# A two-layer graph block on one core: score cross terms without matmuls of their own, and another order of each round

## The reference

```
for k in (0, 1):                       # h starts as x
    a     = softmax(h @ h.T / sqrt(384), axis=-1)
    delta = a * adj
    attn  = delta / (delta.sum(-1, keepdims=True) + 1e-10)
    hl, hs, hr = h @ Wl.T + bl, h @ Ws.T + bs, h @ Wr.T + br
    ctx   = (attn * upper) @ hl + diag(attn)[:, None] * hs + (attn * lower) @ hr
    h     = relu(layernorm(ctx, 1e-12) * gain + shift)
out = layernorm(x + h, 1e-5)
```

## Time and profile before

| | |
|---|---|
| time, median of 3 runs | 1630.99 us (1630.69 to 1631.91) |
| the profiled execution | 1631.82 us, of which 1630.1 from its first to its last instruction (the span) |
| granted clock of TensorE | 0.997 of full speed |
| busy share of the span | PE 98%, PEld 98%, DVE 86%, ACT 66%, POOL 74% |
| DMA | 179 MB in 463,943 packets |

### The profile page before, as it was taken

How to read it: one execution, slowest core, us unless ns; L and a number is a source line. 1 busy time by engine, 2 the same in 40 slices (tenths; PEclk the granted TensorE clock), 3 DMA queues, 4 the chain that set the end, 5 groups by cost and what they waited for, 6 DMA issues and landing times.

```text
span 1630.1 us, 35740 instructions
## 1 busy us (share of the span) xinstructions
PE 1605.1 (98%) x9509; PEld 1597.9 (98%) x9509; DVE 1398.9 (86%) x4368; ACT 1078.0 (66%) x2835; POOL 1212.5 (74%) x1542
## 2 busy tenths in 40 slices
PE   8999999999999999999999999999999999999996
PEld 7899999999999999999999999999999999999995
DVE  7788888888888888888888888888888888888886
ACT  6566666666666666666666666666666666666654
POOL 5677777777777777777777777777777777777764
PEclk9999999999999999999999999999999999999998
DMA  5444444444444444444444444444444444444431
GB/s 175 102 110 107 114 114 107 111 107 116 107 114 111 110 107 113 114 107 112 107 115 106 114 112 110 109 110 115 107 114 109 112 106 114 114 108 111 108 93 45
DMA packets 463943, 179.17 MB, mean 110 GB/s; under 512 B 348592, under 2 KB 462896, under 8 KB 463920
## 3 DMA queue, kind: packets, MB, share of 16 engines
q1 hardware_dynamic: 463920, 178.91, 43.3%
HBM read 112.92 MB, written 65.86 MB: 110 GB/s over the span
## 4 chain that ended last, share of the span: by engine, by line
PE 92%; DMA 1%; DVE 1%; SPq 1%; POOL 1%; ACT 1%; issue 1%; DVEq 0%; POOLq 0%; ACTq 0%
PE p_proj L430 70%; PE p_gather L517 16%; PE p_score L424 5%; PE p_score L446 1%; DMA rows_mem<-rows_blocks 1%; SPq L366 1%; DMA attnT_whole<-attn_mem 1%; SPq L351 0%; POOL rstd L1173 0%; POOL attnT L1163 0%; DVE stats L623 0%; POOL attnT_split L1169 0%; DVE p_gather L646 0%; DVE p_gather L619 0%; DVE rows_blocks L725 0%
## 5 line engine op out<-in xcount | busy, mean ns | idle before, releaser
L430 PE MATMUL p_proj<-w,hT_layer 128*128 128x384 f32 x6912 | 1368.6, 339 | 0.9 <-DVE w L744 0.5
L430 PEld LDWEIGHTS p_proj<-w,hT_layer 128*128 128x128 f32 x6912 | 1162.5, 188 | 2.0 <-POOL w L1220 1.0
L281 POOL TENSOR_TENSOR proj_split<-proj,proj_split 128x768 fp32r<-128x768 f32 x253 | 467.6, 1848 | 182.3 <-ACT proj_split L943 181.9
L517 PE MATMUL p_gather<-proj_split,attnT_split 128*128 128x384 f32 x1536 | 309.3, 335 | 2.3 <-POOL attnT_split L1169 1.6
L1173 POOL TENSOR_TENSOR rstd<-veps,neg_half 128x1 f32<-128x1 f32 x384 | 206.8, 549 | 91.9 <-DVE veps L632 82.6
L517 PEld LDWEIGHTS p_gather<-proj_split,attnT_split 128*128 128x128 f32 x1536 | 269.9, 188 | 4.7 <-POOL attnT_split L1169 2.7
L943 ACT ACTIVATE proj_split<-proj 128x768 fp32r<-128x768 f32 x256 | 214.9, 839 | 84.7 <-DVE proj L688 83.7
L688 DVE TENSOR_TENSOR proj<-p_proj,bias_all 128x768 f32<-128x768 f32 x256 | 244.9, 957 | 12.9 <-PE p_proj L430 5.1
L1169 POOL TENSOR_TENSOR attnT_split<-attnT,attnT_split 128x256 fp32r<-128x256 f32 x256 | 190.3, 743 | 71.0 <-ACT attnT_split L934 70.9
L947 ACT ACTIVATE o<-y,nbias,rstd 128x384 f32<-128x384 f32 x128 | 90.7, 709 | 227.0 <-POOL nbias L1177 227.0
L424 PE MATMUL p_score<-hT_layer 128*128 128x256 f32 x768 | 216.6, 283 | 1.8 <-DVE rows L720 0.8
(11 more groups left out here) (59 smaller groups left out, 1598.3 us busy)
## 6 DMA issues: line engine op xcount, KB each, us to landing
xt_raw<-xT SPq DMA_DIRECT2D x128, 192.0 KB, 2.6
xn<-x SPq DMA_DIRECT2D x128, 192.0 KB, 2.4
out<-o SPq DMA_DIRECT2D x128, 192.0 KB, 2.0
rows_mem<-rows_blocks SPq DMA_DIRECT2D x124, 192.0 KB, 1.9
rowsT<-rows_mem SPq DMA_DIRECT2D x496, 48.0 KB, 2.4
adj_layer<-adj SPq DMA_DIRECT2D x256, 64.0 KB, 1.9
attn_mem<-attn_blocks SPq DMA_DIRECT2D x124, 128.0 KB, 1.7
attnT_whole<-attn_mem SPq DMA_DIRECT2D x496, 32.0 KB, 2.2
```

Source lines behind the costliest of these rows:

```text
L281: op.tensor_tensor(proj_split[u][:, LO], proj[u][:, UP:LOW + 1, :], proj_split[u][:, HI].bitcast(F32), ALU.subtract).then_inc(s_proj_lo[k], 1)
L430: return nc.tensor.matmul(p_proj[:, which, 0:D], hT_of(k, b)[:, slot, st, c, :], w[:, k, which, mv, c, :], start=(n == 0), stop=(n == 8))
L517: last = nc.tensor.matmul(home(k, b)[:, 0:D], AT_split[u][:, st, side, :], proj_split[u][:, mv, side, :], start=(side == UP and n == 0), s ...
```

## The change

TensorE no longer transposes the high-by-low part of the scores. The scores of layer 1 (now of graph i + 2) and of layer 2 (graph i - 2) stand together in its list, one behind each projection step of layer 1's self part (pair_slice), and share one PSUM bank. ScalarE copies both LO parts in one instruction (copy_cross) and both HI parts to free columns of other banks (keep_high). VectorE block-transposes the LO parts of both layers (turn_cross), and they go through DRAM beside the attention of both: the store and the four loads carry four blocks for each row (store_swap, load_swap) instead of two. In the next round GpSimd adds the part and its transpose (add_cross), and then VectorE scales the scores of both layers, one behind the other. The first graphs and the last three of layer 2 keep the cross matmul (11 of 256).

The order of the rounds is another one as well. VectorE adds layer 1's bias ahead of the scaling and layer 2's ahead of the output rows. Layer 2's gather stands nine projection steps later. GpSimd's layer-1 root stands ahead of the cuts. ScalarE has both exponentials behind normalise_rows and ahead of high_sides of layer 2. SP takes xn first and the adjacency tiles last. The input's high and low parts have four slots instead of two, the output's sums, means and roots two instead of one. The core of the diff:

```diff
-        E = [p_score[0][:, 2, :], p_score[1][:, 2, :]]
+        parts = [p_score[0][:, 0:2, :], p_score[0][:, 2:4, :]]
+        cross_parts = p_score[0].rearrange("p (k t) n -> p k t n", t=2)[:, :, LO, :]
+        E = [p_score[1][:, 0, :], p_score[1][:, 1, :]]
         p_rows = bank("p_rows", [P, 4, N])
-        ident_p = [p_score[0][:, 3, :], p_score[1][:, 3, :]]
-        attn_mem = [nc.dram_tensor(f"attn_mem_{slot}", (P, 2, N), F32, kind="Internal").ap() for slot in range(2)]
+        ident_p = p_score[1][:, 2, :]
+        kept = [p_rows[:, 3, :], p_gather[0][:, D:D + N]]
...
+                if b0 is not None and 2 <= n < 2 + C:
+                    step = score_step(0, b0, slot0, n - 2)
+                    if n == 1 + C:
+                        step.then_inc(s_parts[0], 1)
+                if n == 2 + C:
+                    done(pe, s_lo[1], b1)
+                if 2 + C <= n < 2 + 2 * C:
+                    step = score_step(1, b1, slot1, n - 2 - C)
+                    if n == 1 + 2 * C:
+                        step.then_inc(s_parts[1], 1)
...
-                    score0 = (0, i + 1, q) if live(i, i + 1) else None
-                    project_sides(0, i, p, 1, i - 4, range(18), score0)
-                    project_self(0, i, p, 1, i - 4)
+                    b0 = i + 2 if live(i, i + 2) else None
+                    project_sides(0, i, r, 1, i - 4, range(18))
+                    project_self(0, i, r, 1, i - 4, pair=(b0, (r + 2) % 4, i - 2, p))
+                    project_sides(1, i - 3, q, 0, i, range(9))
                     gather(1, i - 4)
-                    project_sides(1, i - 3, q, 0, i, range(18), (1, i - 2, p))
+                    project_sides(1, i - 3, q, 0, i, range(9, 18))
                     project_self(1, i - 3, q, 0, i)
-                    gather(0, i)
+                    gather(0, i, True)
...
+                if live(i, i + 2):
+                    nc.vector.transpose(blocks[:, slot, 2:4].rearrange("p k n -> p (k n)"),
+                                        crossed[:].rearrange("p k n -> p (k n)")).then_inc(s_cross_blocks, 1)
+                else:
+                    nc.vector.transpose(blocks[:, slot, 3], crossed[:, 1]).then_inc(s_cross_blocks, 1)
...
                 low_rows(i - 2, p)
+                add_bias(0, i, True)
+                if not isinstance(i, int) or i > 4:
+                    done(dve, s_cross_sum, i - 5)
+                    done(dve, s_kept, i - 5)
+                    output_mean(i - 5, q)
+                    if live(i, i + 1):
+                        scaled_scores(0, i + 1, q, kept[0], cross_sum[:, 0])
+                    scaled_scores(1, i - 3, q, kept[1], cross_sum[:, 1])
+                if not direct_rows(i, i - 1):
+                    block_rows(i - 1)
+                if live(i, i + 1):
+                    mask(i, 0, i + 1, q)
                 mask(i, 1, i - 3, q)
-                if live(i, i + 1):
-                    done(dve, s_score[0], i + 1)
                 diagonal(1, i - 3, q)
                 if live(i, i + 1):
-                    scaled_scores(0, i + 1, q)
-                add_bias(0, i, True)
-                block_rows(i - 1)
-                if live(i, i + 1):
-                    mask(i, 0, i + 1, q)
                     diagonal(0, i + 1, q)
+                turn_cross(i, p)
                 add_bias(0, i, False)
                 row_moments(1, i - 4, p)
                 row_variance(1, i - 4, p).then_inc(s_veps[1], 1)
                 centre_layer2(i, i - 4)
+                add_bias(1, i - 3, True)
                 output_rows(i - 4, p)
-                done(dve, s_score[1], i - 2)
-                add_bias(1, i - 3, True)
-                scaled_scores(1, i - 2, p)
-                output_mean(i - 4)
                 add_bias(1, i - 3, False)
...
+            def copy_cross(i):
+                if live(i, i + 2):
+                    done(act, s_parts[0], i + 2)
+                    done(act, s_parts[1], i - 2)
+                    nc.scalar.activation(crossed[:], cross_parts, ACT.Copy).then_inc(s_crossed, 1)
+                else:
+                    done(act, s_parts[1], i - 2)
+                    nc.scalar.activation(crossed[:, 1], cross_parts[:, 1], ACT.Copy).then_inc(s_crossed, 1)
+            def keep_high(i):
+                if live(i, i + 2):
+                    nc.scalar.activation(kept[0], parts[0][:, HI, :], ACT.Copy)
+                nc.scalar.activation(kept[1], parts[1][:, HI, :], ACT.Copy).then_inc(s_kept, 1)
...
                 relu_rows(i, i - 2, p)
-                if live(i, i + 1):
-                    cross_scores(0, i + 1)
                 high_rows(i - 2, p)
-                high_sides(1, i - 4)
                 normalise_rows(i, i - 1)
+                exponentials(1, i - 3, q)
                 if live(i, i + 1):
                     exponentials(0, i + 1, q)
+                high_sides(1, i - 4)
+                copy_cross(i)
+                high_projections(0, i)
                 high_sides(0, i)
-                high_projections(0, i)
-                if live(i, i + 2):
-                    high_input(i + 2, p)
+                keep_high(i)
+                if live(i, i + 3):
+                    high_input(i + 3, (r + 3) % 4)
                 if live(i, i + 1):
                     squared_denominators(0, i + 1, q)
                 squared_denominators(1, i - 3, q)
                 if live(i, i - 5):
                     output_squares(i - 5, q)
-                cross_scores(1, i - 2)
-                if live(i, i - 5):
                     finish(i, q)
                 high_projections(1, i - 3)
-                exponentials(1, i - 2, p)
...
+            def add_cross(first, last):
+                nc.gpsimd.tensor_tensor(cross_sum[:, first:last], crossed[:, first:last],
+                                        whole[:, 2 + first:2 + last], ALU.add).then_inc(s_cross_sum, 1)
...
                 low_projections(nc.gpsimd, pool, 1, i - 4)
                 attn_arrived(i - 1, q)
+                if not isinstance(i, int) or i > 4:
+                    add_cross(0, 2)
+                deviation_layer1(i - 1)
                 cut_sides(1, i - 4)
-                deviation_layer1(i - 1)
                 low_sides(1, i - 4)
                 cut_sides(0, i)
                 low_sides(0, i)
                 low_projections(nc.gpsimd, pool, 0, i)
                 deviation_layer2(i - 4)
                 if live(i, i - 5):
-                    deviation_output(i - 5)
-                if live(i, i + 2):
-                    low_input(i + 2, p)
+                    deviation_output(i - 5, q)
+                if live(i, i + 3):
+                    low_input(i + 3, (r + 3) % 4)
...
-                store_attn(i, p)
-                if live(i, i - 3):
-                    done(sp, s_y, i - 5)
-                    sp.dma_start(xn[:, q], x[i - 3]).then_inc(s_xn[q], 16)
+                if not isinstance(i, int) or 3 <= i < G:
+                    store_swap(i, p)
                 if live(i, i - 1) and not direct_rows(i, i - 1):
                     load_rows(i, i - 1, q)
                 if closing(i) and live(i, i - 4):
                     done(sp, s_side[1], i - 4)
-                load_attn(i, p)
+                if not isinstance(i, int) or 3 <= i < G:
+                    load_swap(i, p)
```

More of the change, by code:

```diff
@@ L99, in graph_block @@
         AT_split = [sb(f"attnT_split{k}", [P, 2, 2, N], F32R) for k in (1, 2)]
-        A_blocks = sb("attn_blocks", [P, 2, 2, N])
-        AT_whole = sb("attnT_whole", [P, 2, N])
+        crossed = sb("crossed", [P, 2, N])
+        cross_sum = sb("cross_sum", [P, 2, N])
+        blocks = sb("blocks", [P, 2, 4, N])
+        whole = sb("whole", [P, 4, N])
         rows_blocks = sb("rows_blocks", [P, D])
@@ new lines, in load_swap @@
+            def load_swap(i, slot):
+                first, last = swapped(i)
+                sp.wait_ge(s_swap_out[slot], swap_moves(i, slot))
+                pieces = swap_mem[slot].rearrange("(r a) k (s b) -> s a k r b", a=B, b=B)
+                for s in range(4):
+                    rows_s = slice(s * B, (s + 1) * B)
+                    if last - first == 1:
+                        sp.dma_start(whole[rows_s, first, :].rearrange("a (r b) -> a r b", b=B),
+                                     pieces[s][:, first]).then_inc(s_swap_in[slot], 16)
+                    else:
+                        sp.dma_start(whole[rows_s, first:last, :].rearrange("a k (r b) -> a k r b", b=B),
+                                     pieces[s][:, first:last]).then_inc(s_swap_in[slot], 16)
@@ L464, in project_sides, with project_self @@
                     last.then_inc(s_proj[k], 1)
-            def project_self(k, b, slot, before, b_last, scored=None, first=0, last_part=8):
+            def project_self(k, b, slot, before, b_last, scored=None, first=0, last_part=8, pair=None):
                 done(pe, s_self_biased[before], b_last)
@@ L471, in project_self @@
```

(4 more changed lines are left out.)

334 lines of the change are left out of this document (188 added, 146 removed).

## The result

The changed kernel takes **1697.61 us** (median of 4 runs, 1693.9 to 1699.05), the kernel before 1631.45 beside it (4 runs, 1630.69 to 1633.79): a ratio of 1.040, interval 1.038 to 1.042. It is slower. The profiled execution took 1693.9 us, 62 more than that of before; it is the quickest of the four, so the profile explains these 62 us and not the 66 between the medians.

The account below looks back on a forecast made before the run. TensorE bounds the kernel at 12.44 us a round; relieved to 12.2, it yields to GpSimd's own ring (12.7) and memory's (12.6). Taken as 12.72, +0.28 x 123 = +34.4 on 1631.0 gives 1665 us, range 1612 to 1712.

Parts of the forecast that it names:

- two rings of hand-overs: Waiting chains from one add_cross to the next: GpSimd's own, forecast 12.7 us a round, and one through memory, about 12.6.
- seven of nine: Steps of the ring through memory, from add_cross to the next, forecast to come to about 12.6 us together.
- the ring through memory: add_cross, exponentials, masks, turn_cross, store, loads, landing, next add_cross: forecast 12.3 to 12.7 us, about 12.6, not deciding.
- GpSimd's own: Ring of GpSimd's steps and its waits for ScalarE, add_cross to add_cross: forecast 12.7 us a round, deciding.
- the rival, the alternation of scores and single projections: On TensorE: forecast 0 to 0.2 us a round, taken as 0; as rival in spread_scores 0.1, no chance given.

Follow-up runs that it names:

- finish_only: Changed kernel with only high_projections of layer 2 moved ahead of the output row on ScalarE; 1684.91 us, 1.033 against the kernel before.
- two_row_loads: Changed kernel with two of the four loads of layer 1's rows left out, nothing else; 1649.93 us, 1.011 against the kernel before.
- swap_turn_finish: Changed kernel with layer 1's exponential first (its tile in SBUF), turn_cross ahead of both diagonals, high_projections of layer 2 ahead of the output row; 1610.14 us, 0.988.
- before_no_cross: Kernel before the change with its cross matmuls left out and nothing moved; 1605.16 us, 0.984.
- spread_scores: swap_turn_finish with scores spaced out, layer 1's behind projections 5, 7, 9 of its sides, layer 2's behind 2, 4, 6 of its self part; 1624.74 us, 0.996.

## What to carry to other kernels

When two rings of hand-overs come out within a few per cent of each other, the forecast of which one decides is worth nothing until each hand-over has its own 0.03 to 0.1 us and each transfer the landing for its own size; list them all: here seven of nine erred to the same side. An edit that shortens the ring that doesn't decide is invisible or nearly so (finish_only, 13 us) and worth its full price when the other has been shortened first (42 us): judge such edits together, not one at a time. And when TensorE has no gap, taking work off it pays only as far as the next ring leaves room: look for the in-order waits that make that ring before counting the matmuls.

## What the runs showed of the hardware

- **Landing by size.** Issued in rows of four, loads of 32, 48 and 64 KB, all in pieces of 32 numbers, land 2.2, 2.4 to 2.5 and 2.6 to 2.7 us after their issue. One of 64 KB that follows a pause lands after 2.3 (two_row_loads). The Trainium skill, "DMA: Bandwidth & Descriptors", section "Anatomy of one DMA", has a fit for DMAs that GpSimd issues; taken as an estimate for these, it would give 2.15 at 64 KB. The measured 2.7 decides. With 2.15 the ring through memory would come to 13.0 - 0.56 = 12.4, below GpSimd's own.
- **Issue by size.** In a row of four, SP issues a load every 0.65 to 0.66 us, with 8, 12 or 16 runs for each row alike; a plain transfer, as the store above, takes 0.33.
- **The rate of a stream of matmuls depends on what came before it.** TensorE's timeline in swap_turn_finish: the 18 projections behind a gather last from 816.52 to 819.70, 0.177 each; the 10 behind a score from 813.74 to 815.48, 0.174 each.

```profile
813.74 1.90 PE L464 MATMUL p_proj<-w,hT_layer 128*128 128x384 f32 x10
815.48 1.20 PE L584 MATMUL p_gather<-proj_split,attnT_split 128*128 128x384 f32 x6
816.52 3.34 PE L464 MATMUL p_proj<-w,hT_layer 128*128 128x384 f32 x18
819.70 1.21 PE L584 MATMUL p_gather<-proj_split,attnT_split 128*128 128x384 f32 x6
```

In before_no_cross, where a score follows almost directly behind each gather, 22 projections last from 803.26 to 807.08, 0.174 each:

```profile
803.26 3.99 PE L430 MATMUL p_proj<-w,hT_layer 128*128 128x384 f32 x22
807.08 1.20 PE L515 MATMUL p_gather<-proj_split,attnT_split 128*128 128x384 f32 x6
```

39 projections x 0.003 = 0.12, which is about the gap between the rounds of 12.30 and 12.21. The traces also clear the rival, the alternation of scores and single projections. Scores in a row of alternations, in swap_turn_finish:

```profile
813.33 0.28 PE L458 MATMUL p_score<-hT_layer 128*128 128x256 f32 x1
813.44 0.34 PE L464 MATMUL p_proj<-w,hT_layer 128*128 128x384 f32 x1
813.62 0.28 PE L458 MATMUL p_score<-hT_layer 128*128 128x256 f32 x1
```

and scores two projections apart, in before_no_cross:

```profile
802.67 0.28 PE L424 MATMUL p_score<-hT_layer 128*128 128x256 f32 x1
802.78 0.52 PE L430 MATMUL p_proj<-w,hT_layer 128*128 128x384 f32 x2
803.14 0.28 PE L424 MATMUL p_score<-hT_layer 128*128 128x256 f32 x1
```

From one start to the next, in the mean of the steady rounds, a score takes 0.117 and a projection between two scores 0.177 in the first, 0.118 and 0.178 in the second: the alternation costs nothing. In spread_scores the 18 projections behind a gather again take 0.176 each and the 11 behind a score 0.174. By these spacings its TensorE work, without the wait at the gather, comes to about 12.25 a round (an estimate), 0.05 under swap_turn_finish, as was expected of it; the wait for GpSimd hid that. Why the rate depends on what ran before, no run shows.
